# The last stream of a graph network on one Trainium2 core: ScalarE copies the targets' factors out of PSUM, VectorE weighs from the copy

## The chip, the core and the metric

One core of one Trainium2 chip runs the whole program. The metric is the time of one execution on the device in microseconds (us), the median of several runs. The engines are PE (TensorE's matrix multiplies), PEld (its weight loads), DVE (VectorE), ACT (ScalarE), POOL (GpSimd) and SP (SyncE, which only issues DMAs here). "L2804" is line 2804 of the kernel before.

## The reference

A node table x (6250 nodes, 256 columns) and a graph of 100000 edges sorted by target (`dst`) go through four layers, each added to its input: a graph layer, a gated feed-forward layer, an attention graph layer, and a mixture of eight experts. The last stream holds the second half of the third layer and the whole fourth:

```python
h = (xn @ W).reshape(N, HEADS, HEAD_DIM)            # 8 heads of 32
e = leaky_relu(a_src[src] + a_dst[dst], 0.2)
alpha = exp(e - emax[dst]) / denom[dst]
out = segment_sum(h[src] * alpha[:, :, None], dst) + xn @ W_res + bias
out = layer_norm(out); x = x + out + gelu(out @ ffn_w1 + b1) @ ffn_w2 + b2
# experts, on xn = norm(x):
h = relu(bn(xn @ W1[e] + b1[e])); h = relu(bn(h @ W2[e] + b2[e])); y[e] = h @ Wo[e] + bo[e]
x = x + sum_e y[e] * w[:, e]
```

The exponential of an edge is computed as the larger of two products, each a factor of the source node times a factor of the target node (8 heads, so 16 numbers on either side).

## The kernel before

The nodes are 49 tiles of 128, taken in 13 groups (2, 3, then eleven of 4 tiles). The edges are 196 units of 512 edges (four quarters of 128), three units to a window; each unit runs these steps, named as in the code:

- `gather` (GpSimd, L2766): four indirect DMAs bring 272 columns of each edge's source node, 256 values and 16 source factors, into one of eight slots of `G`.
- `row` (SP): the edges' target numbers, into one of two buffers of `ROW`; `rowhot` (VectorE, L3067): the one-hot matrix `OT` from them, two buffers.
- `factors` (TensorE, L2804): four small matmuls of `OT` with the window's target factors `NDW` give the 16 target factors of each edge in the first 64 columns of PSUM bank 1. There is one such bank, so `factors` of unit i waits until VectorE has read unit i-1.
- `weight` (VectorE): L3083 multiplies the source factors by PB[1] into `E1`, L3086 takes the larger of each pair. Its wait for the gather stands in front of it.
- `weigh` (VectorE, L3092): the 1024 columns of the gathered rows times the weights. `sums` (TensorE, L2793) adds the weighed rows of a window into bank 2, `evac` (ScalarE, L2931) copies the sums out, SP places them in DRAM.

Two more streams share the engines: the node stream (layer norm, the feed-forward layer with `hidden`, `gelu`, `ht_hi`, `ht_lo`, `output`) and the expert stream (`layer` on TensorE, `relu` L3006 and `h_hi` L3014 on ScalarE, `h_lo` L3261 on VectorE, `products` on TensorE, `out_add` L3273 on VectorE). Every matmul of theirs goes through L125; their results rotate over PSUM banks 3, 4 and 6.

Each engine runs a fixed list in order, so a wait holds all that is behind it on that engine. The lists are made before the launch: `last_plan` merges the three streams by their costs (in its step s the edges of group s, the nodes of group s-1 and the experts of group s-2), and `looked_ahead` then schedules the merged list with the costs, lags and needs that `work_of` gives for each step; an engine may take a step from at most 20 (TensorE), 40 (VectorE, ScalarE) or 24 (SP) places ahead. A changed cost or need can so move steps in all lists. The gathers' own order is fixed: unit after unit, each waiting only until its slot is free. In `work_of`:

```python
GATHER, LANDING, LATE = 5.08, 2.1, 2.5
```

Of the kernel before, what the change touches and what calls it, by code (L numbers as in the profile page):

```python
# [14 lines left out]
ACT = mybir.ActivationFunctionType  # L15
AX = mybir.AxisListType

P = 128
# [25 lines left out]
RP = 8  # L44
# [1182 lines left out]
def g_in(S, r):  # L1227
    return (S.g_in0, S.g_in1, S.g_in2, S.g_in3, S.g_in4, S.g_in5, S.g_in6, S.g_in7)[r]
# [993 lines left out]
HOP, DRAIN, SWAP, SPARE = 0.06, 0.15, 1.28, 0.1  # L2222
# [21 lines left out]
def work_of(tok, slot_of):  # L2244
# [4 lines left out]
    def add(engine, what, us, needs, gives=None, lag=0.0, **more):  # L2249
        out.append(Work(engine, what, us, lag, tuple(n for n in needs if n), what if gives is None else gives, **more))  # L2250

    if step == "weight":
        j, = x
        add("POOL", ("gather", j), GATHER, [j >= RP and ("sums", (j - RP) // 3)], lag=LANDING)
        add("DVE", tok, 0.44, [("gather", j), ("factors", j)])
    elif step == "weigh":
        add("DVE", tok, 1.14, [("weight", x[0])])
    elif step == "onehot":
        j, = x
        add("DVE", tok, 0.2, [j >= RL and ("sums", (j - RL) // 3)])  # L2260
    elif step == "rowhot":
        j, = x
        add("DVE", tok, 0.28, [("row", j), j >= 2 and ("factors", j - 2)])
    elif step == "row":
        j, = x
# [3 lines left out]
        add("SP", tok, 2.6, [w >= RN and ("factors", last_unit(w - RN))], lag=6.0)  # L2269
    elif step == "factors":  # L2270
        i, = x
        add("PE", tok, 0.14, [("rowhot", i), ("window", i // 3)], lag=DRAIN, bank=1, frees=("weight", i))
    elif step == "sum":
        j, = x
        w = j // 3
# [46 lines left out]
    elif step == "node":  # L2322
        g, i, k = x
# [5 lines left out]
    elif step in ("mom_b", "mom2_b"):  # L2329
        g, = x  # L2330
        a, root = ("mom_a", "root") if step == "mom_b" else ("mom2_a", "root2")
# [36 lines left out]
    elif step == "prepare":  # L2368
# [16 lines left out]
        elif s in (5, 6) and LGROUPS[g][2 * (s - 5):2 * (s - 5) + 2]:  # L2385
            add("PE", ("bo", g, s), 0.22 * len(LGROUPS[g][2 * (s - 5):2 * (s - 5) + 2]), [("share_out", g)], lag=DRAIN, bank="turn",
                frees=("bo_add", g, s))
# [28 lines left out]
    elif step == "products":  # L2416
# [3 lines left out]
            frees=("out_add", it, h))  # L2420
# [99 lines left out]
def last_alloc(nc, sb):  # L2520
    b = Bag()
    b.MW = sb("MW", [P, RQ, 2, 512], F32R)
    b.XR = sb("XR", [P, RX, D])
    b.AR = sb("AR", [P, RA, D])
    b.G = sb("G8", [P, RP, 4, 272])
    b.OR2 = sb("OR2", [P, RL, 4, Q])
    b.OT = sb("OT", [3 * Q, 2, 512], BF16)
    b.ROW = sb("ROW", [3 * Q, RO, 512], BF16)
    b.NDW = sb("NDW", [3 * Q, RN, 4, 16], BF16)
    b.WIN = sb("WIN2", [P, RV, 264])  # L2530
    b.SUMS = [sb("SUMa", [P, 2, 264]), sb("SUMb", [P, 2, 264])]
    b.E1 = sb("E1", [P, 4, 16])
    b.fb1 = sb("gb1", [P, 8])
    b.g2c = sb("g2c", [P, 2])
    b.g2r = sb("g2r", [P, D])
    b.b2c = sb("b2c", [P, 2])
    b.RI = sb("RI", [P, 2, D])
    b.RD = sb("RD", [P, 4, 8])
    b.TY = sb("TY9", [P, 512])
    b.YT = [sb("YT9h", [P, 2, 512], F32R), sb("YT9l", [P, 2, 512], F32R)]  # L2540
    b.TF = sb("TF9", [P, 2, 256])
    b.HT = [sb("HT9h", [P, 3, 256], F32R), sb("HT9l", [P, 3, 256], F32R)]
    b.WRs = sb("WRs", [P, 16])
    b.WRr = sb("WRr", [P, 2, 2, 8], F32R)
    b.brr = sb("brr", [P, 8])
    b.BO3 = sb("BO3", [24, D], F32R)
    b.bom = sb("bom", [24, 2])
    b.SCL = sb("SCL", [P, 2, 16])
    b.BIA = sb("BIA", [P, 2, 16])
    b.YM = sb("YtM", [P, 4, D])  # L2550
    b.YMT = [sb("YTMh", [P, 2, 2, 512], F32R), sb("YTMl", [P, 2, 2, 512], F32R)]
    b.H = [[sb("H1h", [P, 2, 512], F32R), sb("H1l", [P, 2, 512], F32R)],
           [sb("H2h", [P, 2, 512], F32R), sb("H2l", [P, 2, 512], F32R)]]
    b.TM = sb("TFm", [P, 2, 512])
    b.CV = b.TM[:, 1, 256:416].rearrange("p (a n) -> p a n", a=10)
    b.LG = sb("LG", [P, 4, 8])
    b.LM = sb("LM", [P, 4])
    b.WE = sb("WE", [P, 2, 4, 8])
    b.W3 = sb("W3", [P, 4, 24], F32R)
    b.WTr = sb("WTr", [24, 512], F32R)  # L2560
    return b
# [53 lines left out]
def general_second(nc, c, G, A):  # L2615
    st = ExitStack()
    b = general_second_alloc(nc, lambda n, s, dt=F32: st.enter_context(nc.sbuf_tensor(n, s, dt)))
    v = nc.vector

    nc.sync.dma_start(b.ACC[:, :, :], nodes(c.tab1)[:, :, 0:256]).then_inc(G.own, 16)  # L2620
    v.wait_ge(G.own, 16)
    for t in range(NT):
        hk = b.ACC[:, t, :].rearrange("p (h d) -> p h d", h=8)
        v.tensor_tensor(hk, hk, c.DEN[:, t, :].unsqueeze(2).to_broadcast([P, 8, 32]), ALU.mult)
    nc.all_engine_barrier()
    dst = general_targets(nc, c, b, G, A)
    with nc.Fori(0, NG) as g:
        general_source_pool(nc.gpsimd, c, b, G, g, b.G[:, 0, :], c.tab1)
        own = Own(v, G.step)
        own.done(v.tensor_copy(b.RL[:, 0:1], dst[:, bass.ds(g, 1)]))  # L2630
        own.done(v.tensor_scalar(b.RL[:, 1:2], b.RL[:, 0:1], float(NP - 1), None, ALU.min))
        v.tensor_copy(b.IX[:, 1:2], b.RL[:, 1:2]).then_inc(G.onehot, 1)
        general_second_factors_pool(nc.gpsimd, c, b, G)
        nc.all_engine_barrier()
        nc.gpsimd.sem_clear(G.step)
        nc.all_engine_barrier()
        general_second_weights(v, c, b, G)
        nc.all_engine_barrier()
        nc.gpsimd.sem_clear(G.step)
        nc.all_engine_barrier()  # L2640
        with nc.Fori(0, NT) as t:
            general_second_dve_tile(v, c, b, G, t)
            general_second_pe_tile(nc.tensor, c, b, G)
            nc.all_engine_barrier()
            nc.gpsimd.sem_clear(G.onehot)
            nc.gpsimd.sem_clear(G.sum)
            nc.all_engine_barrier()
    nc.sync.dma_start(nodes(c.accd), b.ACC[:, :, :]).then_inc(G.out, 16)
    nc.sync.wait_ge(G.out, 16)
    nc.all_engine_barrier()  # L2650
    st.close()
# [118 lines left out]
def last_pe(nc, c, b, S, plan):  # L2770
    pe, PB = nc.tensor, c.PB
    on = Awaited(pe)
# [11 lines left out]
    for step, *x in plan["PE"]:  # L2784
# [11 lines left out]
        elif step == "factors":  # L2796
            i, = x
            on.wait_ge(S.rowhot, i + 1)
            if i:
                on.wait_ge(S.factor, i)  # L2800
            w = i // 3
            on.wait_ge(nd_in(S, w % RN), 64 * (w // RN + 1))
            for u in range(4):
# [112 lines left out]
def last_act(nc, c, b, S, plan):  # L2916
    a, PB = nc.scalar, c.PB
    on = Awaited(a)
    bank_of = rounds_of(plan)
    for step, *x in plan["ACT"]:  # L2920
        if step == "deviation":
            on.wait_ge(S.bn_var, 2)
            for l in range(2):
                var = b.CV[:, 5 * l + 4, :]
# [130 lines left out]
def last_dve(nc, c, b, S, plan, fast):  # L3055
    v, PB = nc.vector, c.PB
    on = Awaited(v)
# [13 lines left out]
    for step, *x in plan["DVE"]:  # L3071
# [6 lines left out]
        elif step == "weight":  # L3078
            j, = x
            on.wait_ge(g_in(S, j % RP), 64 * (j // RP + 1))  # L3080
            on.wait_ge(S.nd_mm, j + 1)
            on.wait_ge(own.sem, weights_done)
            v.tensor_tensor(b.E1[:, :, :], b.G[:, j % RP, :, 256:272], PB[1][:, 0:64].rearrange("p (u c) -> p u c", u=4),  # L3083
                            ALU.mult).then_inc(S.factor, 1)
            on.wait_ge(S.factor, j + 1)
            own.mark(v.tensor_tensor(b.G[:, j % RP, :, 256:264], b.E1[:, :, 0:8], b.E1[:, :, 8:16], ALU.max))  # L3086
# [1 line left out]
        elif step == "weigh":  # L3088
            j, = x
# [4 lines left out]
        elif step == "onehot":  # L3094
            j, = x
# [28 lines left out]
        elif step == "node":  # L3124
            g, i, k = x
# [88 lines left out]
        elif step == "logit":  # L3214
# [4 lines left out]
            sums = PB[bank_of["router", g]][:, 0:16 * L].rearrange("p (i e) -> p i e", e=16)  # L3219
# [70 lines left out]

def last_layers(nc, c, A, out):
    S = named(nc, c, "last", "dve consts g_in0 g_in1 g_in2 g_in3 g_in4 g_in5 g_in6 g_in7 nd_in0 nd_in1 nd_in2 nd_in3 row_in0 row_in1 rowhot onehot "
                             "nd_mm factor product edge_mm evac placed sum_in0 sum_in1 sums self_in0 self_in1 self_in2 self_in3 "
                             "weighed_self x_in0 x_in1 res_in0 res_in1 res_add var std rows scaled kept rows_t rows_out rows_hi rows_lo "
                             "hid gelu ht_hi ht_lo out_ffn taken xvar xstd bn_var bn_std affine router xrows xrows_t "
                             "xrows_hi xrows_lo logit_mm logit centred expd share share_t share_out bo_mm bo_add "
                             "mw_in0 mw_in1 mw_in2 mw_in3 mw_in4 mw_in5 h1_mm h2_mm h1_relu h2_relu h1_hi h2_hi h1_lo "
                             "h2_lo out_mm out_add shared stored0 stored1 stored2 stored_end")
    G = named(nc, c, "lastg", "row onehot sum step own out")

    def body(fast):
        plan = last_plan(fast)
        if not fast:
            nc.sync.wait_ge(c.nd_out, 32)
            nc.all_engine_barrier()
            general_second(nc, c, G, A)
        st, way = ExitStack(), "" if fast else "_general"
        b = last_alloc(nc, lambda n, s, dt=F32: st.enter_context(nc.sbuf_tensor(n + way, s, dt)))
        if fast:
            last_pool(nc, c, b, S)  # L3310
        last_sp(nc, c, b, S, A, plan, fast, out)
        last_pe(nc, c, b, S, plan)
        last_act(nc, c, b, S, plan)
        last_dve(nc, c, b, S, plan, fast)
        st.close()

    nc.all_engine_barrier()
    both_ways(nc, c, body)


def named(nc, c, phase, names):

    names = names.split()
    sems = namedtuple("Sems_" + phase, names)(*[nc.alloc_semaphore(name=f"{phase}_{n}") for n in names])
    c.done_with.extend(sems)
    return sems
# [130 lines left out]
```

## Time and profile before

| | |
|---|---|
| median of 3 runs (lowest to highest) | 2821.39 us (2816.93 to 2828.64) |
| the profiled execution | 2827.59 us |
| its span, first to last instruction | 2825.9 us |
| busy in the span: PE, DVE, ACT, POOL | 2275.7, 1926.8, 1339.6, 1884.6 us |
| mean granted TensorE clock | 0.881 of full |

The span leaves 1.7 us of the profiled execution outside it. The last stream's gathers begin at 1306 us of the span, its last one is issued at 2570 us. An engine's busy share is an average over stages with different limits, so the stretches are to be read one by one; a busy PE row says that matmuls were in flight, not that they ran at peak.

### The profile page before, as it was taken

Reading aid. Unit: us, or ns where it says so; the run is one execution under the profiler, and the core shown is the slowest. Engines: PE = TensorE matmul, PEld = TensorE weight load, DVE = VectorE, ACT = ScalarE, POOL = GpSimd, SP = SyncE. Lnnn points to the kernel's source line nnn. Section 1 sums busy time; section 2 is a strip of 40 time slices with the busy share of each in tenths; the row PEclk is TensorE's granted clock in tenths of the full one; section 3 lists DMA queues with packets and bytes.
Section 4 is the critical chain, followed back from the end, with each engine's and each line's share of the span. In section 5 each row is a group of like instructions: output and inputs, shape, how many; then the busy total and the mean of one; then the engine's idle time right before and its main releaser. Section 6 shows DMA issues by size and latency. Waiting matters only on the chain. (4 is left out here: it accounts for less than half of the span.)

```text
span 2825.9 us, 50094 instructions
## 1 busy us (share of the span) xinstructions
PE 2275.7 (81%) x16869; PEld 1899.2 (67%) x16869; DVE 1926.8 (68%) x5122; ACT 1339.6 (47%) x2771; POOL 1884.6 (67%) x1695
## 2 busy tenths in 40 slices
PE   8557777567766777683368889999999999999998
PEld 7435555456555556673157778888788888888887
DVE  9844445445345546784577778988988988988754
ACT  7313333233333335342135546666666756656765
POOL 7277777777777772574778888887878877883000
PEclk9578788788988878696579989999999999999999
DMA  9554444444444441068678787887877887876444
GB/s 331 170 157 137 133 129 137 138 126 138 137 136 133 130 122 53 30 194 217 199 214 264 234 252 225 258 271 222 275 231 242 263 243 246 268 227 208 159 139 128
DMA packets 312862, 531.09 MB, mean 188 GB/s; under 512 B 89678, under 2 KB 210321, under 8 KB 312597
## 3 DMA queue, kind: packets, MB, share of 16 engines
q1 hardware_dynamic: 234021, 312.19, 34.9%
q0 software_dynamic: 75264, 212.04, 26.4%
q10 hardware_dynamic: 3312, 3.55, 0.4%
q8 instruction: 139, 2.28, 0.3%
q14 instruction: 126, 1.03, 0.1%
HBM read 454.05 MB, written 73.54 MB: 187 GB/s over the span
## 5 line engine op out<-in xcount | busy, mean ns | idle before, releaser
L2766 POOL DMA_INDIRECT G<-tab,SRCL x784 | 1002.6, 1279 | 282.6 <-issue 253.2
L1194 POOL DMA_INDIRECT GE<-tab,SRCL x748 | 728.0, 973 | 237.4 <-issue 210.2
L3006 ACT ACTIVATE TFm<-PB,BIA,SCL 128x512 f32<-128x512 f32 (+2 forms) x416 | 312.8, 753 | 335.1 <-PE PB L125 304.2
L1257 PE MATMUL PB<-GE,OR 128*32 128x257 f32 x1496 | 145.4, 465 | 271.1 <-issue 270.7
L125 PE MATMUL PB<-MW,H2h 128*128 128x256 f32 x1568 | 289.2, 284 | 8.6 <-DVE H2l L3261 8.6
L125 PE MATMUL PB<-H1h,MW 128*128 128x512 f32 (+2 forms) x832 | 285.3, 396 | 4.6 <-DVE H1l L3261 2.5
L125 PE MATMUL PB<-YTMh,MW 128*128 128x512 f32 (+2 forms) x832 | 286.5, 397 | 0.0
L125 PEld LDWEIGHTS PB<-MW,H2h 128*128 128x128 f32 x1568 | 245.7, 190 | 15.8 <-issue 7.0
L1257 PEld LDWEIGHTS PB<-GE,OR 128*32 128x32 f32 x1496 | 36.0, 118 | 324.9 <-issue 321.3
L3092 DVE TENSOR_TENSOR G<-G 128x1024 f32<-128x1024 f32 x196 | 237.8, 1214 | 0.6
L1040 DVE TENSOR_TENSOR OR<-iotaf,REL 128x128 f32<-128x128 f32 x392 | 105.4, 285 | 183.1 <-PE PB L1257 171.2
L125 PE MATMUL PB<-MW,H2l 128*128 128x256 f32 x784 | 220.4, 281 | 0.0
L1578 ACT ACTIVATE TF<-PB,fb 128x256 f32<-128x256 f32 (+1 forms) x200 | 93.7, 470 | 197.0 <-PE PB L125 174.5
L3273 DVE SCALAR_TENSOR_TENSOR XR<-PB,WE,XR 128x256 f32<-128x256 f32 x392 | 169.9, 475 | 22.6 <-PE PB L125 21.8
L125 PEld LDWEIGHTS PB<-H1h,MW 128*128 128x128 f32 x832 | 158.1, 192 | 39.6 <-issue 8.4
L1509 DVE TENSOR_TENSOR HTl<-TF,HTh 128x256 fp32r<-128x256 f32 (+1 forms) x200 | 82.1, 419 | 148.0 <-ACT HTh L1586 146.5
L125 PEld LDWEIGHTS PB<-YTMh,MW 128*128 128x128 f32 x832 | 158.4, 193 | 35.3 <-issue 8.0
L3261 DVE TENSOR_TENSOR H2l<-TFm,H2h 128x512 fp32r<-128x512 f32 (+2 forms) x208 | 134.8, 653 | 51.5 <-ACT H2h L3014 50.9
L3261 DVE TENSOR_TENSOR H1l<-TFm,H1h 128x512 fp32r<-128x512 f32 (+2 forms) x208 | 134.5, 653 | 42.8 <-ACT H1h L3014 42.1
L125 PE MATMUL PB<-H1l,MW 128*128 128x512 f32 (+2 forms) x416 | 160.8, 387 | 0.0
L125 PE MATMUL PB<-YTMl,MW 128*128 128x512 f32 (+2 forms) x416 | 160.7, 386 | 0.0
L125 PEld LDWEIGHTS PB<-MW,H2l 128*128 128x128 f32 x784 | 148.9, 190 | 0.0
(365 smaller groups left out, 6507.6 us busy)
## 6 DMA issues: line engine op xcount, KB each, us to landing
MW<-msplit SPq DMA_DIRECT2D x312, 512.0 KB
ROW<-relrow SPq DMA_DIRECT2D x196, 96.0 KB
msplit<-FWs SPq DMA_DIRECT2D x68, 256.0 KB
part<-ZERO SPq DMA_DIRECT2D x2, 6600.0 KB
G<-tab,SRCL POOLq DMA_INDIRECT x784
GE<-tab,SRCL POOLq DMA_INDIRECT x748
part<-WIN SPq DMA_DIRECT2D x262, 33.0 KB
SUMa<-part SPq DMA_DIRECT2D x49, 132.0 KB
```

Source lines behind the costliest of these rows:

```text
L125: ins = pe.matmul(ps, lhs(p), rhs(q), start=(first and i == 0), stop=(last and i == 2), skip_group_check=True)
L1040: return v.tensor_tensor(to, c.iotaf[:, 0:Q].unsqueeze(1).to_broadcast([P, 4, Q]), c.REL[:, 4 * u:4 * u + 4].unsqueeze(2).to_broadcast([P, ...
L1194: po.indirect_dma_start(c.GE[:, (s - 2 * UE) % RU, q, 0:256], None, c.tab0, bass.IndirectOffsetOnAxis(ap=c.SRCL[:, 2 * s + q:2 * s + q + 1 ...
L1257: ins = pe.matmul(PB[w % 2][Q * q:Q * q + Q, 0:257], b.OR[:, u % RH, q, :], rows, start=first, stop=last)
L1509: v.tensor_tensor(b.HT[1][:, q % 3, 0:n], b.TF[:, q % 2, 0:n], b.HT[0][:, q % 3, 0:n].bitcast(F32), ALU.subtract).then_inc(S.ht_lo, 1)
L1578: a.activation(b.TF[:, q % 2, 0:n], PB[bank][:, 0:n], ACT.Gelu_apprx_tanh, bias=b.fb1[:, m:m + 1]).then_inc(S.gelu, 1)
L2766: po.indirect_dma_start(b.G[:, j % RP, u, :], None, c.tab1, bass.IndirectOffsetOnAxis(ap=c.SRCL[:, 4 * j + u:4 * j + u + 1].bitcast(U32), ...
L3006: a.activation(b.TM[:, m, 0:n], PB[of][:, 0:n], ACT.Relu, bias=b.BIA[:, l, q:q + 1], scale=b.SCL[:, l, q:q + 1]).then_inc(S.h2_relu if l e ...
L3092: v.tensor_tensor(row, row, b.G[:, j % RP, :, 256:264].unsqueeze(3).to_broadcast([P, 4, 8, 32]), ALU.mult).then_inc(S.product, 1)
L3261: v.tensor_tensor(b.H[l][1][:, m, 0:n], b.TM[:, m, 0:n], b.H[l][0][:, m, 0:n].bitcast(F32), ALU.subtract).then_inc(S.h2_lo if l else S.h1_ ...
L3273: v.scalar_tensor_tensor(out=XR[:, x_slot(k), :], in0=PB[OUTS[h]][:, D * i:D * i + D], scalar=b.WE[:, g % 2, 2 * h + i, e:e + 1], in1=XR[: ...
```

## The change

ScalarE gets a step `factor_out` of each unit: it copies the 64 columns of bank 1 into one of two SBUF buffers `FS`. VectorE's `weight` waits for that copy and reads `FS` in place of PSUM; TensorE's next `factors` waits for the copy in place of VectorE's multiply; the copy waits until VectorE has read the buffer two units before. `work_of` states the new needs, puts 0.19 us for the copy on ScalarE, and 0.40 us in place of 0.44 for `weight`.

```diff
@@ -2252,7 +2252,7 @@
     if step == "weight":
         j, = x
         add("POOL", ("gather", j), GATHER, [j >= RP and ("sums", (j - RP) // 3)], lag=LANDING)
-        add("DVE", tok, 0.44, [("gather", j), ("factors", j)])
+        add("DVE", tok, 0.4, [("gather", j), ("factor_out", j)])
     elif step == "weigh":
         add("DVE", tok, 1.14, [("weight", x[0])])
     elif step == "onehot":
@@ -2269,7 +2269,8 @@
         add("SP", tok, 2.6, [w >= RN and ("factors", last_unit(w - RN))], lag=6.0)
     elif step == "factors":
         i, = x
-        add("PE", tok, 0.14, [("rowhot", i), ("window", i // 3)], lag=DRAIN, bank=1, frees=("weight", i))
+        add("PE", tok, 0.14, [("rowhot", i), ("window", i // 3)], lag=DRAIN, bank=1, frees=("factor_out", i))
+        add("ACT", ("factor_out", i), 0.19, [tok, i >= 2 and ("weight", i - 2)])
     elif step == "sum":
         j, = x
         w = j // 3
@@ -2530,6 +2531,7 @@
     b.WIN = sb("WIN2", [P, RV, 264])
     b.SUMS = [sb("SUMa", [P, 2, 264]), sb("SUMb", [P, 2, 264])]
     b.E1 = sb("E1", [P, 4, 16])
+    b.FS = sb("FS", [P, 2, 64])
     b.fb1 = sb("gb1", [P, 8])
     b.g2c = sb("g2c", [P, 2])
     b.g2r = sb("g2r", [P, D])
@@ -2797,7 +2799,7 @@
             i, = x
             on.wait_ge(S.rowhot, i + 1)
             if i:
-                on.wait_ge(S.factor, i)
+                on.wait_ge(S.factor_out, i)
             w = i // 3
             on.wait_ge(nd_in(S, w % RN), 64 * (w // RN + 1))
             for u in range(4):
@@ -2918,7 +2920,13 @@
     on = Awaited(a)
     bank_of = rounds_of(plan)
     for step, *x in plan["ACT"]:
-        if step == "deviation":
+        if step == "factor_out":
+            i, = x
+            on.wait_ge(S.nd_mm, i + 1)
+            if i >= 2:
+                on.wait_ge(S.factor, i - 1)
+            a.copy(b.FS[:, i % 2, :], PB[1][:, 0:64]).then_inc(S.factor_out, 1)
+        elif step == "deviation":
             on.wait_ge(S.bn_var, 2)
             for l in range(2):
                 var = b.CV[:, 5 * l + 4, :]
@@ -3078,9 +3086,9 @@
         elif step == "weight":
             j, = x
             on.wait_ge(g_in(S, j % RP), 64 * (j // RP + 1))
-            on.wait_ge(S.nd_mm, j + 1)
+            on.wait_ge(S.factor_out, j + 1)
             on.wait_ge(own.sem, weights_done)
-            v.tensor_tensor(b.E1[:, :, :], b.G[:, j % RP, :, 256:272], PB[1][:, 0:64].rearrange("p (u c) -> p u c", u=4),
+            v.tensor_tensor(b.E1[:, :, :], b.G[:, j % RP, :, 256:272], b.FS[:, j % 2, :].rearrange("p (u c) -> p u c", u=4),
                             ALU.mult).then_inc(S.factor, 1)
             on.wait_ge(S.factor, j + 1)
             own.mark(v.tensor_tensor(b.G[:, j % RP, :, 256:264], b.E1[:, :, 0:8], b.E1[:, :, 8:16], ALU.max))
@@ -3290,7 +3298,7 @@
 
 def last_layers(nc, c, A, out):
     S = named(nc, c, "last", "dve consts g_in0 g_in1 g_in2 g_in3 g_in4 g_in5 g_in6 g_in7 nd_in0 nd_in1 nd_in2 nd_in3 row_in0 row_in1 rowhot onehot "
-                             "nd_mm factor product edge_mm evac placed sum_in0 sum_in1 sums self_in0 self_in1 self_in2 self_in3 "
+                             "nd_mm factor factor_out product edge_mm evac placed sum_in0 sum_in1 sums self_in0 self_in1 self_in2 self_in3 "
                              "weighed_self x_in0 x_in1 res_in0 res_in1 res_add var std rows scaled kept rows_t rows_out rows_hi rows_lo "
                              "hid gelu ht_hi ht_lo out_ffn taken xvar xstd bn_var bn_std affine router xrows xrows_t "
                              "xrows_hi xrows_lo logit_mm logit centred expd share share_t share_out bo_mm bo_add "
```

## Rows read from the trace of the kernel before

**Rows 1.** The page's busy times of the whole span

```profile
PE 2275.7 (81%) x16869; PEld 1899.2 (67%) x16869; DVE 1926.8 (68%) x5122; ACT 1339.6 (47%) x2771; POOL 1884.6 (67%) x1695
```

**Rows 2.** Stretches: us, PE, PEld, DVE, ACT, POOL busy, clock, DMA share, GB/s

```profile
1306.00:1400.00 94.00, 18.54 (x188) 8.02 (x188) 45.45 (x132) 3.70 (x9) 72.50 (x70) 0.52 0.74 200
1400.00:1713.00 313.00, 254.01 (x1970) 217.10 (x1970) 236.58 (x663) 155.94 (x309) 250.52 (x206) 0.87 0.79 239
1713.00:2571.00 858.00, 846.05 (x6354) 718.19 (x6355) 753.33 (x1964) 543.57 (x927) 679.24 (x510) 1.00 0.82 250
2571.00:2826.00 255.00, 240.23 (x1556) 210.90 (x1554) 151.42 (x352) 156.95 (x261) 0.39 (x1) 0.99 0.44 139
```

**Rows 3.** TensorE's waits, 1713 to 2571: us, times, longest

```profile
PE PB L125 <- DVE YT9l L3174: 5.3, 4, 2.2
PE PB L125 <- DVE H1l L3261: 1.9, 2, 1.0
PE PB L125 <- DVE H2l L3261: 1.6, 2, 1.3
```

**Rows 4.** TensorE's waits, 1400 to 1713

```profile
PE PB L2804 <- DVE E L3083: 14.0, 8, 4.6
PE PB L2804 <- issue: 13.4, 6, 3.3
PE PB L2814 <- DVE YtM L130: 7.9, 3, 3.7
PE PB L125 <- DVE HT9l L3182: 6.8, 5, 4.6
```

**Rows 5.** VectorE's longest wait, 1400 to 1713

```profile
DVE E L3083 <- DMA G<-tab,SRCL: 42.4, 20, 7.0
```

**Rows 6.** Timeline of VectorE, then of TensorE, around 1528

```profile
1527.76 0.22 DVE L3083 TENSOR_TENSOR E<-G,PB 128x64 f32<-128x64 f32 x1 [3.34 <-DMA G<-tab,SRCL]
...
1528.13 0.24 PE L2804 MATMUL PB<-NDW,OT 96*128 96x16 bf16 x4 [3.54 <-DVE E L3083]
```

**Rows 7.** GpSimd's waits for TensorE, 1400 to 1713, then 1713 to 2571

```profile
POOL G L2766 <- PE PB L2793: 0.3, 1, 0.3
...
POOL G L2766 <- PE PB L2793: 28.8, 17, 5.9
```

**Rows 8.** Timeline of VectorE, last multiplies that waited for a gather

```profile
1689.51 0.22 DVE L3083 TENSOR_TENSOR E<-G,PB 128x64 f32<-128x64 f32 x1 [7.04 <-DMA G<-tab,SRCL]
...
1713.06 0.22 DVE L3083 TENSOR_TENSOR E<-G,PB 128x64 f32<-128x64 f32 x1 [2.47 <-DMA G<-tab,SRCL]
```

**Rows 9.** The chain that ended last, one step of six matmuls

```profile
2301.51 1.49 PE PB L125 x6
```

**Rows 10.** ScalarE's copies out of PSUM: ns min/median/max

```profile
L1803 ACT COPY AD<-PB x49: 173/178/182, 1187.1 to 1292.4; 128x16 f32<-128x16 f32 x49
...
L2931 ACT COPY WIN<-PB x66: 359/379/383, 1328.2 to 2629.9; 128x264 f32<-128x264 f32 x66
```

**Rows 11.** ScalarE's longest wait, 1713 to 2571

```profile
ACT TFm L3006 <- PE PB L125: 189.8, 167, 4.9
```

**Rows 12.** VectorE by shape, 1700 to 2570: busy us, mean ns

```profile
L1040 DVE TENSOR_TENSOR OR<-iotaf,REL 128x128 f32<-128x128 f32 x125 | 31.3, 280 | 0.1
L3083 DVE TENSOR_TENSOR E<-G,PB 128x64 f32<-128x64 f32 x127 | 27.2, 214 | 13.0 <-PE PB L2804 8.9 <-DMA G<-tab,SRCL 2.5 <-issue 0.6
L3086 DVE TENSOR_TENSOR G<-E 128x32 f32<-128x32 f32 x127 | 24.9, 196 | 4.4
...
L3166 DVE TENSOR_TENSOR XR<-XR,AR 128x256 f32<-128x256 f32 x34 | 13.0, 422 | 0.6
...
L3189 DVE TENSOR_TENSOR XR<-PB,XR 128x256 f32<-128x256 f32 x32 | 12.0, 415 | 8.5 <-PE PB L125 8.5
```

## The prediction

> **What bounds the kernel now.** I read the page's busy times first, then the last stream by stretch, then who waited for whom in each. Over the whole span PE is busy 81%, the others less [rows 1]; that average hides three limits [rows 2]. From 1713 to 2571 PE is busy 846.05 of 858 us at the full clock (2.4 GHz) and idle 12.0; from 2571 to the end it is idle 14.8 of 255. So after 1713 the end is set by PE's work, and all that any other engine could give back there is 26.7 us. What PE waits for in that stretch are low halves and turned rows from VectorE, 5.3, 1.9 and 1.6 us as the longest [rows 3]; no wait of the `factors` step L2804 is among them.
>
> From 1400 to 1713 it is different: PE is busy 254.01 of 313 us, idle 59.0, and its clock is 0.87 of full, a mixture of its two levels [rows 2]. Here the longest waits are those of L2804: 14.0 us put down to the multiply L3083, and 13.4 us put down to "issue" [rows 4]. The second line is the first one again: its waits come directly behind a multiply that ended. Together 27.4 us, 14 times. This is what the change takes hold of. But the multiply itself is late: VectorE stood 42.4 us in 20 waits for the gathered rows [rows 5]. One pair shows the mechanism: the multiply at 1527.76 had waited 3.34 us for the gather, and PE's `factors` at 1528.13 had stood 3.54 us for that multiply [rows 6]. And GpSimd, which issues the gathers, waited 0.3 us for a free slot in the whole stretch [rows 7]: it issues one after the other without pause. So up to 1713 gathers set the pace, and PE's stall is the shadow of theirs. The last multiplies held by one are at 1689.51 (7.04 us) and 1713.06 (2.47 us) [rows 8]. After 1713 GpSimd waits 28.8 us for slots [rows 7], so the gathers are ahead and PE is the bound.
>
> **The change, part by part.**
>
> *PE no longer waits for the multiply* (removes up to 27.4 us of waits before 1713). When VectorE stands for a gather, PE may now run past `factors`. But the steps behind it need low halves that the same VectorE makes, in order, behind the multiply. And what PE gains is waited out again at the next multiply that stands for its rows, the last time at 1713.06, whose time is the gather's. What passes that point is what PE can have done ahead of VectorE: with three rotating banks one or two steps, of 1.49 us each [rows 9]. I take one: -1.5 us; bounds 0 and, if all the wait came back, -27.4.
>
> *The copy on ScalarE.* Not in the trace. Two copies of other widths are: 16 columns out of PSUM take 178 ns, 264 take 379 [rows 10]; on the line between them 64 columns take 178 + 48 x 201/248 = 217 ns. 196 x 0.217 = 42.5 us of ScalarE. From 1713 to 2571 there are some 127 units [rows 12], 27.6 us more on an engine that is busy 543.57 of 858 [rows 2] and whose `relu` waits 189.8 us for PE [rows 11]. That idle time hides the copy; were it gone, each would cost its 0.217 us. A copy counts only where it stands in front of a `relu` whose matmuls have just ended and PE has no other step ready. ScalarE's load grows by 5% of itself; if PE's 12.0 us of waits grow in that proportion, it is 0.6 us. I take +1, bounds 0 and +27.6. The copy is also a new link between `factors` and the multiply, 0.2 us and a handoff; the multiply of a unit follows its `factors` by most of a unit's 858/127 = 6.8 us where it runs ahead, so nothing.
>
> *The wait in ScalarE's queue.* The copy of unit i waits until VectorE has read unit i-2. Behind it stand `relu`, `h_hi` and `gelu`, and behind these VectorE's low halves and PE's three banks. Before 1713 VectorE stands for a gather at such a moment anyway, and PE with it: nothing. After 1713 gathers come early, and the reading of unit i-2 lies two units back: nothing in the forecast, and the slower rival below.
>
> *The multiply from SBUF.* Now 214 ns out of PSUM with 64 columns. From SBUF alone 32 columns take 196 and 128 take 280; on the line between, 64 take 224 [rows 12]. Adds of 256 columns agree: 415 ns with a PSUM source, 422 without. Bounds per multiply: -18 ns (as cheap as 32 columns) and +10; x 196 = -3.5 and +2.0 us on VectorE, which is not the bound after 1713 (753.33 of 858 busy) [rows 2]. I take 0. The Trainium skill ("Perfetto Trace Analysis", section "Optimizing Scalar/DVE Operations") gives about 60 ns of access overhead on SBUF against 125 on PSUM for VectorE, which would be 196 x 65 ns = 12.7 us (an estimate from that page); the 415 and 422 ns rows don't show it. Another page speaks against the change: "VectorE: DVE Perf Modes", section "Rules for kernel authors", has one copy a matmul's output out of PSUM first if many operations follow, and here a single one does.
>
> *Multiplies that waited for `factors`*, 8.9 us from 1713 on [rows 12]: with a second buffer these should shrink. VectorE's time, hidden under PE: 0.
>
> *The order.* Costs and needs of `work_of` change, so all five lists are planned anew, SP's rows, windows and placements too. The merge of the streams is not touched, so how much expert and node work stands before the unit at 1713 (near number 67: 196 less the 127 from 1700 on [rows 12] and the few after 2570) stays, but for the few steps of the lookahead. I can't cost a new order step by step. Its bounds: it could halve the 26.7 us of idle after 1713 (-13), or double it (+27). I take 0.
>
> Sum: -1.5 + 1 + 0 = -0.5 us against the profiled 2827.6 (span 2825.9 and 1.7 outside). That execution is 6.2 us above the median of the runs, 2821.4, so the forecast for the median is 2821 us.
>
> **The rivals.**
>
> *The wait comes back on ScalarE (slower).* Place: ScalarE's list after 1713, a copy in front of a `relu`. For it: VectorE is busy 753.33 of 858 us there, so a multiply can run late, and the copy passes its lateness to the engine that frees PE's banks. Against: PE's own waits are only 12.0 us, and ScalarE idles 314. If each of 127 copies costs its 0.217 us, +27.6: 2849 us. It decides (0.5%, which is 14.1 us, about what a measurement of this kernel can tell from no change) once 0.11 us a unit are lost.
>
> *PE's stalls come back as time (faster).* For it: 27.4 us of direct waits, at a clock of 0.87 whose loss is up to 0.13 x 313 = 41 us of work. The Trainium skill ("Perfetto Trace Analysis", section "Matmul Optimizations") says the engine scales its power with use and wants matmuls back to back; the 0.52 and 0.87 beside 1.00 [rows 2] agree. Against: the gathers' pace, rows 5, 7 and 8. It needs later steps to be planned in front of the unit at 1713. If the whole wait returns: -27.4, 2794 us; if half, 2807.
>
> *The new order by itself.* Either sign: to 2808 at best, 2848 at worst, worked out above.
>
> *VectorE is relieved (faster).* Even 12.7 us less on VectorE would end in PE's bound: with PE's waits shrinking in that proportion (12.7 of 753), under 1 us. No case of its own.
>
> **How the numbers follow.** Forecast, within 0.5%: 0.52. Stalls come back by more than 14 us: 0.17. A better order by more than that: 0.08. ScalarE's queue: 0.13. A worse order: 0.10. So faster 0.25, same 0.52, slower 0.23. The forecast's own range is 2807 to 2835. The wide one reaches to 2800, half-way to the whole wait's 2794, and to 2843, short of the rivals' 2848, and leaves out a tenth on either side.
>
> **What the new profile would show.** Right: L2804's waits for L3083 gone before 1713; the waits of the multiply for gathers as long as before or longer (over 42 us); the last one held near 1713; PE about 98.6% busy after it; copies of about 217 ns; a multiply still at 214 to 224 ns. Wrong: the last gather-held multiply clearly earlier in the work, with more expert matmuls before it (the stalls were real time); waits of PE for ScalarE or for low halves above some 25 us after 1713, and `relu` waiting behind copies (the slower rival); or a PE that waits for steps far from the edges (the order).

## The result, and the profile after

The changed kernel takes 2847.35 us (median of 4 runs, 2839.40 to 2850.71) where the kernel before took 2820.14 beside it (4 runs, 2816.93 to 2828.64). The ratio is 1.0087, interval 1.0072 to 1.0102: slower, by more than the 0.5% that this kernel's measurement can tell, and 4 us beyond the upper end of the range. The forecast was no change.

The profiled execution of the changed kernel is the lowest of its runs (2839.40 us, span 2837.5), and that of before was on the high side (2827.59), so the two traces differ by 11.6 us of span where the medians differ by 27. The last stream's first gather starts at 1306.47 before and at 1302.95 after. From there to the end, with the columns of [rows 2], first before, then after:

```profile
1306.47:2825.90 1519.43, 1358.83 (x10066) 1154.20 (x10066) 1186.31 (x3107) 860.15 (x1505) 1002.65 (x784) 0.94 0.74 226
1302.95:2837.50 1534.55, 1363.74 (x10066) 1152.41 (x10066) 1193.97 (x3107) 881.68 (x1701) 894.24 (x784) 0.94 0.73 224
```

The stream takes 15.1 us more: with the same 10066 matmuls PE is idle 170.8 us in place of 160.6, and busy 4.9 us more. The slowdown lies in this stream; the rest of the 27 us lies in how far each of these two executions is from its median.

The page of the changed kernel, busy times of the whole span (against [rows 1]):

```profile
PE 2259.3 (80%) x16869; PEld 1879.7 (66%) x16869; DVE 1934.7 (68%) x5122; ACT 1361.1 (48%) x2967; POOL 1774.2 (63%) x1695
```

196 more instructions on ScalarE are the copies, and all the rest is the same in number. PE's busy time is 16 us less over the whole span, but all of that, and more, comes from ahead of the stream. POOL's busy time fell by 110 us: the mean gather took 1.28 us before and 1.14 after, though no gather was edited. These are the page's groups of gathers, first before, then after (busy, mean ns, idle):

```profile
L2766 POOL DMA_INDIRECT G<-tab,SRCL x784 | 1002.6, 1279 | 282.6 <-issue 253.2
```

```profile
L2768 POOL DMA_INDIRECT G<-tab,SRCL x784 | 894.2, 1141 | 394.3 <-issue 251.4
```

By stretch, changed kernel, with the columns of [rows 2]:

```profile
1400.00:1713.00 313.00, 259.30 (x2033) 221.05 (x2034) 250.49 (x689) 168.71 (x374) 246.19 (x220) 0.90 0.81 252
1713.00:2571.00 858.00, 835.63 (x6232) 705.00 (x6230) 735.29 (x1901) 537.91 (x1020) 572.59 (x494) 0.99 0.78 243
```

The surprise is in both rows. Up to 1713 the changed kernel is ahead: 63 matmuls more, 5.3 us more of PE's work, 14 gathers more (220 against 206). Part of it is only that its stream began 3.5 us earlier: over the first 400 us from its first gather PE is busy 269.7 us against 266.2, and 268.9 in a second trace of the same kernel. After 1713 it loses: PE idles 858 - 835.63 = 22.4 us where it idled 12.0, and issues 122 matmuls fewer.

What PE, VectorE and ScalarE waited for from 1400 to 1713 in the changed kernel (us, times, longest):

```profile
ACT FS L2928 <- DVE E L3091: 22.7, 13, 4.1
...
DVE E L3091 <- DMA G<-tab,SRCL: 20.2, 11, 4.4
PE PB L2806 <- ACT FS L2928: 17.2, 11, 4.8
...
PE PB L2806 <- issue: 7.3, 2, 4.0
```

PE's wait for the multiply is gone by name [rows 4] and stands there again as a wait for the copy: 17.2 + 7.3 = 24.5 us in place of 27.4. The first row says why: the copy itself waits 22.7 us for the multiply of two units before, which waits for its gather. `factors` of unit i waits for the copy of i-1, and that for the multiply of i-3, where it waited for the multiply of i-1 before: PE runs two units further and then meets the same stall. The wait for gathers fell, from 42.4 us [rows 5] to 20.2, and to 33.0 in the second trace.

PE's waits from 1713 to 2571 in the changed kernel:

```profile
PE PB L2795 <- DVE G L3100: 5.4, 4, 2.0
PE PB L2816 <- DVE YtM L130: 4.1, 3, 1.7
PE PB L125 <- DVE H2l L3269: 3.6, 3, 1.4
PE PB L125 <- DVE H1l L3269: 3.2, 4, 2.1
PE PB L2806 <- ACT FS L2928: 3.2, 8, 0.4
```

Only the last row belongs to the new copy: 3.2 us in 8 waits, 0.4 the longest. The 10 us more of idle time are spread: 5.4 us more for the weighed rows that `sums` reads, 3.2 for the copy, and 2.6 more for the normalized rows that L2816 turns. The waits for low halves, all kinds together, are 6.8 us where they were 10.2 before. Except for the copy, these are waits between steps that nobody edited.

The copy and the multiply by themselves, changed kernel (ns min/median/max):

```profile
L2928 ACT COPY FS<-PB x196: 193/212/233, 1312.8 to 2630.4; 128x64 f32<-128x64 f32 x196
L3091 DVE TENSOR_TENSOR E<-G,FS x196: 163/216/274, 1313.7 to 2630.7; 128x64 f32<-128x64 f32 x196
```

212 ns against the 217 predicted, and a multiply that is no cheaper out of SBUF: the median is 216 ns, and it was 215 out of PSUM. The edited instructions cost what the sum said. So the question was: the mechanism's wait on ScalarE, or the order of the lists?

### The profile page after: what moved, and what is told of

Read it like the earlier page. It is cut to its first block, busy times and chain, and to the rows that moved or that the text cites. A ratio compares the mean times of both kernels' runs of the same rounds, so it can differ in the third digit from the quotient of the medians.

```text
span 2837.5 us, 50674 instructions
## 1 busy us (share of the span) xinstructions
PE 2259.3 (80%) x16869; PEld 1879.7 (66%) x16869; DVE 1934.7 (68%) x5122; ACT 1361.1 (48%) x2967; POOL 1774.2 (63%) x1695
## 4 chain that ended last, share of the span: by engine, by line
PE 35%; DVE 6%; POOL 4%; DMA 4%; issue 3%; SPq 1%; ACT 0%; DVEq 0%; POOLq 0%; ACTq 0%
PE PB L125 30%; POOL G L2768 4%; PE PB L2795 2%; DMA ROW<-relrow 1%; DVE G L3100 1%; DMA SUMb<-part 1%; DMA G<-tab,SRCL 1%; DVE XR L3281 1%; DVE H2l L3269 1%; DVE H1l L3269 1%; DMA RI<-resd 0%; SPq L2678 0%; PE PB L2806 0%; DVE YtM L130 0%; DVE AR L3139 0%
## 5 line engine op out<-in xcount | busy, mean ns | idle before, releaser
L2768 POOL DMA_INDIRECT G<-tab,SRCL x784 | 894.2, 1141 | 394.3 <-issue 251.4
L125 PEld LDWEIGHTS PB<-YTMh,MW 128*128 128x128 f32 x832 | 158.4, 193 | 40.6 <-issue 12.3
L3269 DVE TENSOR_TENSOR H1l<-TFm,H1h 128x512 fp32r<-128x512 f32 (+2 forms) x208 | 134.2, 653 | 42.3 <-ACT H1h L3022 41.3
```

Of the source, the lines that this page charges most:

```text
L125: ins = pe.matmul(ps, lhs(p), rhs(q), start=(first and i == 0), stop=(last and i == 2), skip_group_check=True)
L2768: po.indirect_dma_start(b.G[:, j % RP, u, :], None, c.tab1, bass.IndirectOffsetOnAxis(ap=c.SRCL[:, 4 * j + u:4 * j + u + 1].bitcast(U32), ...
L3269: v.tensor_tensor(b.H[l][1][:, m, 0:n], b.TM[:, m, 0:n], b.H[l][0][:, m, 0:n].bitcast(F32), ALU.subtract).then_inc(S.h2_lo if l else S.h1_ ...
```

## The experiments

Each was timed beside the kernel before on the same chip, and each ratio is to that. There were two kinds of chips. On some the kernel before took 2820 to 2825 us, as above. On three others it took 3287, 3254 and 3345 us, and there all comparisons came out otherwise; those runs have a part of their own below.

The lists can be compared without the chip. Of the steps in each list, so many stand in the same place as in the kernel before, and the last column is the end that the planner computes for the lists that it chose:

```
                                    PE of 1380  DVE of 2017  planner's end
before                                                          1458.0 us
the changed kernel                      534          406        1487.5
before, 0.40 for `weight`              1022         1168        1471.6
before, 0.48 for `weight`               701          590        1494.1
changed, 0.44 for `weight`              603          421        1491.4
```

The changed kernel thus has two changes in one: a mechanism (a copy, its buffer, its waits) and another order of most of the lists.

### The mechanism in the order of before

`work_of` as before, so the lists are planned as before, and the copy is put into ScalarE's list where `factors` has ended; buffer, waits and multiply as in the changed kernel.

```diff
+    if any(work.step[0] == "factors" for t, work, needs in log):
+        log = with_copies(log)
...
+def with_copies(log):
+    out = [(t, work, needs) for t, work, needs in log]
+    for t, work, needs in log:
+        if work.step[0] == "factors":
+            out.append((t + work.us + work.lag, Work("ACT", ("factor_out", work.step[1]), 0.2, 0.0, (), None), ()))
+    return sorted(out, key=lambda x: x[0])
```

> The kernel of e1_old_order (mechanism of the change, lists of the kernel before) once more, since there the kernel before itself took 3287 us in place of 2820 and engines stood for microseconds with no releaser. If the kernel before is at 2815 to 2830 us here: order theory 0.997 to 1.003, mechanism theory 1.006 to 1.010.

Measured: 2826.06 us, ratio 0.9997 (0.9985 to 1.001; 10 runs, 13 of before). Its stretches:

```profile
1400.00:1713.00 313.00, 252.29 (x1968) 216.48 (x1969) 235.37 (x660) 162.06 (x361) 250.49 (x206) 0.88 0.78 238
1713.00:2571.00 858.00, 846.49 (x6347) 716.97 (x6347) 751.89 (x1957) 556.19 (x1049) 672.61 (x509) 1.00 0.81 250
```

These are [rows 2] again to within 2 us of PE in each stretch, the 206 gathers included. From 1400 to 1713 VectorE waits for gathers, and PE for VectorE's low halves, where it waited for the multiply [rows 4]:

```profile
DVE E L3101 <- DMA G<-tab,SRCL: 56.0, 28, 5.1
PE PB L125 <- DVE HT9l L3200: 12.6, 7, 3.9
PE PB L125 <- DVE H2l L3279: 11.0, 6, 3.6
```

In this stretch PE waits for the copy once, 1.6 us, and is idle as long as before, 60.7 us against 59.0. This is the prediction's reading: the stall is that of the gathers, and passes on to the steps behind. ScalarE's waits, 1713 to 2571:

```profile
ACT TFm L3024 <- PE PB L125: 112.2, 113, 2.8
ACT FS L2938 <- PE PB L2816: 97.9, 67, 4.5
```

ScalarE stands 97.9 us in front of a copy, head of line, far more than the 41.3 in the changed kernel, and it costs nothing: the `relu` behind it used to wait 189.8 us [rows 11] and now waits 112.2. The waiting has changed its name. In this order the mechanism costs nothing and brings nothing.

### Four buffers for the copies

```diff
-    b.FS = sb("FS", [P, 2, 64])
+    b.FS = sb("FS", [P, 4, 64])
...
-            if i >= 2:
-                on.wait_ge(S.factor, i - 1)
+            if i >= 4:
+                on.wait_ge(S.factor, i - 3)
```

(and `% 4` in both indices; lists of the changed kernel.)

> The kernel of e3_four_buffers (the changed kernel's lists, four copy buffers) once more, for the same reason. Theory that the copy's wait for its buffer is what costs: 1.000 to 1.004. Order theory: 1.007 to 1.010.

Measured: 2842.81 us, 1.0065 (1.0048 to 1.0082); PE idles 21.3 us from 1713 to 2571, against 22.4 with two buffers. The copy's wait for its buffer was 72.5 us over the whole stream with two buffers, and is gone with four. The median is 2.7 us lower than that of the changed kernel timed beside it (2845.52, below), which the intervals don't tell from nothing. This wait is not the cause.

### The changed kernel again

No edit; it stands beside the others on their chip.

> The changed kernel itself, so that the others stand beside it on the same chip, and for a second profile of it: 1.007 to 1.010 by both theories, and again some 22 us of idle TensorE between 1713 and 2571 where the kernel before has 12.

Measured: 2845.52 us, 1.0078 (1.0061 to 1.0095); PE idles 23.9 us from 1713 to 2571. The loss is there again.

### Another order, and nothing else

The kernel before with one number of its planner changed. No instruction is added, removed or altered.

```diff
-        add("DVE", tok, 0.44, [("gather", j), ("factors", j)])
+        add("DVE", tok, 0.48, [("gather", j), ("factors", j)])
```

> The kernel of e5_before_048 (no instruction added, lists planned with 0.48 us for weight; the planner's own end 1494.7 against 1458.0 before) once more. Order theory: 1.008 to 1.013. Mechanism theory: within 0.2% of 1.000.

Measured: 2809.1 us, 0.9942 (0.9926 to 0.9959): faster, though its planner's end is the latest of all. An order alone moves the time, but the expectation had the sign wrong: it had taken the planner's end for a guide. Its stretches:

```profile
1400.00:1713.00 313.00, 266.70 (x2121) 229.08 (x2121) 253.06 (x705) 168.11 (x336) 247.47 (x216) 0.90 0.81 249
1713.00:2571.00 858.00, 848.54 (x6359) 719.73 (x6358) 749.18 (x1951) 536.98 (x928) 604.71 (x500) 1.00 0.80 249
```

12.7 us more of PE's work before 1713 than in [rows 2], as the changed kernel also had in part, and 9.5 us of idle after it: this order keeps what it gained. The same with 0.40, the changed kernel's cost for `weight`:

> The kernel of h2 and j2 (no instruction added, lists planned with 0.40 for weight), once more. With the kernel before near 2825 us: order theory off 1.000 by more than 0.15%, either sign; mechanism theory within 0.2%. With it at 3250 us or more: again 1.018 to 1.029.

Measured: 2829.97 us, 1.002 (1.0004 to 1.0036). That is the border of both expectations and decides nothing between them; it does show that the cost of 0.40 by itself is not the loss of 0.87%.

### The changed kernel with the old cost

All instructions and needs of the changed kernel; only its planner has 0.44 again. 581 of 1380 steps of PE and 506 of 2017 of VectorE stay in the places of the changed kernel's lists; 895 and 993 stand where the order of 0.48, the fast one, has them.

```diff
-        add("DVE", tok, 0.4, [("gather", j), ("factor_out", j)])
+        add("DVE", tok, 0.44, [("gather", j), ("factor_out", j)])
```

> The kernel of h3 and j3 (the changed kernel with only the planner's cost of weight back at 0.44), once more. With the kernel before near 2825 us: order theory anywhere from 0.995 to 1.012 but not the changed kernel's 1.008; if the new needs as such spoil every order, 1.006 to 1.010. With it at 3250 us or more: again 1.03 to 1.04.

Measured: 2820.49 us, 0.998 (0.9966 to 0.9994). The loss is gone, with every copy and every wait still in the code. Its stretches:

```profile
1400.00:1713.00 313.00, 264.42 (x2105) 226.67 (x2106) 251.62 (x698) 173.08 (x386) 245.81 (x220) 0.92 0.81 250
1713.00:2571.00 858.00, 839.38 (x6281) 710.10 (x6280) 747.64 (x1935) 544.06 (x1039) 578.69 (x495) 1.00 0.81 248
```

### The mechanism in the fast order

The first experiment, but planned with 0.48.

> The kernel of h1 and j1 (the faster order of f3_before_048 with the whole mechanism of the change in it), a third time. If the kernel before is near 2825 us: order theory 0.994, within 0.003; copies that cost something, 0.998 or more. If it is at 3250 us or more: again 1.030 to 1.035, above the 1.0255 that this order had there without copies.

Measured: 2808.39 us, 0.9947 (0.9926 to 0.9968), the same as the order of 0.48 alone. The mechanism is free in a second order; this version and the one without copies beat both kernels.

### The chips on which the kernel before takes 3250 to 3345 us

The mechanism in the order of before (before: 3287.09 us on this chip):

> The whole mechanism of the change (copy on ScalarE, two buffers, VectorE reads the copy, TensorE waits for the copy), but the lists of TensorE, VectorE, SP and GpSimd are those of the kernel before, step by step, and ScalarE's is the old one with each copy put in at the place where its factors are ready in the plan. Theory O (the new order costs the time): the ratio to the kernel before is 1.000, within 0.997 to 1.003 (2812 to 2829 us). Theory M (the copy, its wait or its handoff costs the time whatever the order): 1.006 to 1.010 (2837 to 2848 us), as the changed kernel's 1.0087.

Measured 3342.23 us, 1.0129 (1.0017 to 1.024). The cost of 0.40:

> The kernel before with nothing changed but the planner's cost of the step weight, 0.40 in place of 0.44 (the figure that the change puts there); no instruction is added. About a quarter of the steps of TensorE's list and over a third of VectorE's change place. Theory O: slower than before though nothing but the order differs, 1.002 to 1.008; the planner's own end of its list is 1471.6 against 1458.0 for the kernel before and 1487.5 for the changed one, so if that order of ends holds, half of the changed kernel's loss, 1.004. Theory M: 1.000, within 0.2%.

Measured 1.0218 (1.0135 to 1.03). Four buffers:

> The changed kernel with four buffers for the copy in place of two, all lists as in the changed kernel: ScalarE's copy of unit i no longer waits for VectorE's reading of unit i-2 but of i-4, so the 72.5 us that it stood for it vanish. Theory M in its form 'the wait comes back in ScalarE's queue': most of the loss returns, ratio 1.000 to 1.004. Theory O: unchanged, 1.007 to 1.010.

Measured 1.0466 (1.0407 to 1.0525). The cost of 0.48:

> The kernel before with the planner's cost of weight at 0.48 in place of 0.44, no instruction added. The planner's own end of its list is 1494.7, above the changed kernel's 1487.5. Theory O: as slow as the changed kernel or slower, 1.008 to 1.013 (2843 to 2857 us). Theory M: 1.000, within 0.2%.

Measured 1.0255 (1.0171 to 1.0338). None of these four came as expected. Taken alone, they would say that the copies cost 1.3% and every new order 2%. PE's waits of the first, 1700 to 3100, say that something else was going on there:

```profile
PE PB L125 <- issue: 92.8, 78, 6.8
PE PB L125 <- ACT TFm L3024: 21.3, 8, 5.0
```

PE stands 92.8 us in 78 waits for nothing that the profile shows. VectorE's and ScalarE's instructions take the same time as before (the 128x1024 multiply 1215 ns against 1214, `relu` 754 against 753), but PE's costliest matmuls take 5% longer by the mean (298, 419 and 417 ns against 284, 396 and 397), at a mean clock of 0.83 in place of 0.88. The stages ahead of the stream, which nobody edited, are slower too: in the first 1300 us PE issues 6013 matmuls where it issued 6803. On two more such chips the later kernels gave the same picture. Before: 3254.08 us,

> The faster order of f3_before_048 (lists of the kernel before as planned with 0.48 for weight) with the whole mechanism of the change in it: the copies put into ScalarE's list where their factors are ready, two buffers, VectorE reads the copy. Order theory (the copy is free, only the order counts): 0.994, as f3 without copies, within 0.003. If the copies cost something that the first order hid by chance: 0.998 or more.

> The kernel of e2_before_040 (no instruction added, lists planned with 0.40 for weight, planner's own end 1471.6) once more, off the chip on which the kernel before took 3287 us. Order theory: off 1.000 by more than the noise of 0.15%, either sign, since f3 showed that the planner's end doesn't tell the sign. Mechanism theory: within 0.2%.

> The changed kernel with only the planner's cost of weight put back to 0.44: same instructions, same new needs, another order (about 40% of the steps of TensorE's and 25% of VectorE's stay in place). Order theory: clearly another time than the changed kernel's 1.008, anywhere from 0.995 to 1.012. If the new needs as such spoil every order: 1.006 to 1.010 again.

measured 1.0313 (1.0229 to 1.0397), 1.0284 (1.0191 to 1.0378) and 1.0405 (1.0297 to 1.0512). A fourth kernel on the chip of 3254 us had the changed kernel's mechanism and a table of shifts (the planner's offsets by kind of step, lines 2225 to 2229) searched anew for it, by the planner's own end, which fell to 1463.6:

```diff
-    ("ACT", "evac"): -70, ("ACT", "gelu"): -60, ("ACT", "ht_hi"): 30, ("ACT", "rows_hi"): 30, ("ACT", "xrows_hi"): 50,
...
+    ('ACT', 'evac'): -5,
+    ('ACT', 'gelu'): -5,
+    ('ACT', 'ht_hi'): -5,
...
```

> The changed kernel with the planner's table of shifts searched anew for the changed costs and needs, so that its own end falls from 1487.5 to 1463.6 (before: 1458.0). Instructions as in the changed kernel. If the old table no longer fitting is the cause and the planner's end is of use within one set of needs: 0.998 to 1.002. If the planner's end says nothing: as likely at 1.008 as below.

Measured 1.0533 (1.0448 to 1.0618), the slowest of all with the earliest planner's end of the new plans. It was run on that chip alone, so what it does on the others is open. And with before at 3344.67 us:

> The kernel of h1_048_order_copy (the faster order of f3_before_048 with the whole mechanism of the change in it) once more, off the chips on which the kernel before took 3250 us and more. If the kernel before is near 2825 us here: order theory 0.994, within 0.003; if the copies cost something, 0.998 or more.

> The kernel of h2_before_040 (no instruction added, lists planned with 0.40 for weight) once more. Order theory: off 1.000 by more than 0.15%, either sign. Mechanism theory: within 0.2%.

> The kernel of h3_after_044 (the changed kernel with only the planner's cost of weight back at 0.44) once more. Order theory: clearly another time than the changed kernel's 1.008, anywhere from 0.995 to 1.012. If the new needs as such spoil every order: 1.006 to 1.010.

measured 1.0329 (1.0278 to 1.038), 1.0186 (1.0128 to 1.0244) and 1.0333 (1.0286 to 1.038). On the chips where before takes 2824 us the same three kernels gave 0.9947, 1.002 and 0.998. Why every other kernel loses there isn't settled. Those with copies lose more by the medians (1.0313 and 1.0329 against 1.0255 in the order of 0.48, 1.0129 in that of before), but the intervals overlap, the last one begins at 1.0017, and the pairs in the order of 0.48 were timed on different chips, so that copies cost something on these chips is neither shown nor excluded. The explanation below is that of the chips with 2820 to 2825 us, where the change itself was timed.

## Why the prediction was wrong

**What the loss is.** All the kernels, with PE's idle time in the last stream's two long stretches (from windows as above), the last multiply that had waited for a gather (VectorE's timeline, 1560 to 1800), and the stream from its first gather to the end, all from one execution each:

```
                         idle 1400-1713  1713-2571   sum   last held   stream    ratio
0.48 order                       46.3        9.5     55.8    1587      1503.7   0.9942
0.48 order + copies              44.3       12.9     57.2    1579      1500.5   0.9947
changed, cost 0.44               48.6       18.6     67.2   < 1560     1517.2   0.998
before                           59.0       12.0     70.9    1713      1519.4   1
before, cost 0.40                56.5       15.0     71.5    1702      1530.0   1.002
old order + copies               60.7       11.5     72.2    1711      1525.5   0.9997
the changed kernel               53.7       22.4     76.1    1663      1534.6   1.0087
changed, four buffers            56.2       21.3     77.5    1674      1536.1   1.0065
the changed kernel again         57.8       23.9     81.7    1682      1535.2   1.0078
```

The windows are fixed while the streams begin between 1301 and 1307 us, so a single column is good to a few us. The sums, and the streams, go nearly as the ratios do. The 0.48 order idles 15 us less than before and is 16 us faster; the changed kernel idled 5 and 11 us more in its two traces and is 27 and 21 us slower, its stream 15 and 16 us longer. After 2571 PE idles 3.5 us more again (18.2 us, against 14.7). Single executions spread by some 10 us. The copy's presence doesn't sort this table: two kernels with copies stand above before and one at its side.

**How far that shows the cause.** Without copies, two orders gave 0.9942 and 1.002. With copies and all their waits, four gave 0.9947, 0.9997, 0.998 and 1.0087. In the two orders that ran both ways, the copies changed nothing beyond the intervals. So the loss needs the order that the changed kernel's plan came to. It doesn't add up from parts: the new cost alone gave +0.2%, the new needs alone -0.2%, both together +0.87%. One kernel is missing: the changed kernel's order without its copies. It can't run, for the lists would stand in a circle. VectorE has `rowhot` of unit 7 in front of `weight` of unit 4; without the copy `factors` of unit 5 waits for that `weight`, and `rowhot` 7 waits for `factors` 5. So it isn't excluded that the loss needs this order and the copy's waits together. Of such waits 3.2 us could be seen on PE after 1713, and taking the largest of ScalarE's away, with four buffers, gave nothing clear of noise.

**Point by point.**

- *"The order ... I can't cost a new order step by step ... I take 0"*, with +27 as its bound and 0.10 as the chance of a worse one: this is the step that failed. The order was worth 16 us one way (0.48, no copies), and the order of the changed kernel 27 the other, with the open end above. With no instruction changed the time went from 0.9942 to 1.002; with the instructions of the change, from 0.9947 to 1.0087. The rival and its price (2848) were written down, and then the range was cut at 2843, below it. That price was met by luck: it had the 26.7 us of idle after 1713 double, and they became 40.6. The bound on the other side, -13, was too narrow: the 0.48 order gained 12.7 us of PE's work before 1713, while the bound had counted only idle time after 1713.
- *"What passes that point ..., whose time is the gather's"*: wrong as well, outside the old order. The last multiply held by a gather was taken for a fixed point at 1713. In the lists of before all the signs of "right" came, with the copies in place: 56.0 us of waits for gathers, the last at 1711.09, PE 98.7% busy after 1713 (846.49 of 858), copies of 212 ns. The reading of the waits was sound for the old lists and was carried over to new ones. The last multiply held lies at 1713 and 1711 in the two kernels with the order of before, and at 1702, 1682, 1674, 1663, 1587, 1579 and before 1560 in the others. Under "wrong" the text named this sign, and it came, as this row of VectorE's timeline in the changed kernel shows (start, us, what; in brackets what it had waited for), with nothing of the kind between 1690 and 1800:

```profile
1663.22 0.23 DVE L3091 TENSOR_TENSOR E<-G,FS 128x64 f32<-128x64 f32 x1 [4.40 <-DMA G<-tab,SRCL]
```

  PE's time before 1713 could be won, but it didn't come from the wait that the change took hold of, since the order of 0.48 wins more of it without the copy (12.7 us against 5.3). The gather's own time was no fixed thing either: from 1400 to 1713 GpSimd issues without a pause in both kernels, 206 gathers before (250.52 / 206 = 1.22 us each) and 220 after (1.12 us). Counted from the first gather, the changed kernel's multiply of unit 60 (the first is unit 0) started 13.0 us earlier than before's, that of unit 80 21.3 us earlier, that of unit 150 7.2 us later and that of unit 180 11.7 later. The lead was given back after 1713.
- *The copy on ScalarE*: right. 212 ns, 196 times, hidden behind `relu`'s wait for PE; the cost over all is -0.03% (-0.15 to 0.1) in the order of before, and in that of 0.48 the ratio went from 0.9942 to 0.9947.
- *The wait in ScalarE's queue*, and the rival made of it: set at nothing, and nearly so. Its sign was a PE waiting for ScalarE above 25 us after 1713; it was 3.2. The time of 2849 that this rival gave was met by chance, by another cause.
- *The multiply from SBUF*: right. The medians are 216 ns in the changed kernel, 224 in the old order with copies, 215 before. The Trainium skill ("Perfetto Trace Analysis", section "Optimizing Scalar/DVE Operations") gives SBUF some 65 ns less than PSUM; these rows don't show it at 64 columns. The Trainium skill would copy a matmul's output out of PSUM first only for many operations ("VectorE: DVE Perf Modes", section "Rules for kernel authors"); here, with one, the copy was neither harm nor gain in the two orders that ran both ways.
- *PE no longer waits for the multiply*: right that the direct wait is worth about nothing. In the old order it came back as waits for low halves, as the text had it. In the changed kernel 24.5 us of it came back through the copy's own wait for its buffer, which the text had set at nothing before 1713.
- *"PE about 98.6% busy after it"*: 835.63 / 858 = 97.4% in the changed kernel, where 98.7% came in the old order with copies.

**What stays open.** Which exchanged steps cost the 10 us after 1713 wasn't found: the waits that grew stand in many places, 5.4 us at the most. Why the gathers run faster in some orders (mean 1.28 us before, 1.18 and 1.15 in two others, 1.14 in the changed kernel) is also open. Before 1713 GpSimd waits at most 2.3 us for slots in any of them, so there it is no matter of slots. But most of the difference lies after 1713, and there short gathers and waits for slots go together: 1.33 us each with 28.8 us of waits for a slot [rows 7] before, 1.16 us with 141.4 in the changed kernel, 1.21 with 83.5 in the order of 0.48. Which brings which isn't shown.

## What to carry to other kernels

Where a change touches the costs or needs of a planner that lays out static lists, it is two changes: time the mechanism in the old lists, and time a new order with no instruction altered, before either is judged. If a cost moved by 9% alone changes the time by 0.6%, a change of that size says nothing about its mechanism. The planner's own end was no guide: its latest (1494.1) was the fastest kernel, and the changed kernel with the cost of 0.44 ran 1% faster than the changed kernel, at a later end (1491.4 against 1487.5). So it is worth nothing that it ranked before and the changed kernel rightly.

## What the runs showed of the hardware that was not expected

- The same indirect gathers, with the same bytes, took 1.28 us on average before and 1.18 with another order of the other engines' work and nothing else changed; with copies as well, 1.28 in the old order and 1.14 to 1.17 in the others.
- One kernel took 2820 to 2825 us on some chips and 3254 to 3345 on others. There VectorE's and ScalarE's instructions took the same time, matmuls 5% more by the mean, and PE stood up to 6.8 us at a time for nothing that the profile shows. A ratio from such a chip didn't carry over: 1.0255 there was 0.9942 elsewhere.
- ScalarE waited 97.9 us at the head of its queue and it cost nothing (0.9997), since what stood behind would have waited anyway.
